# Two causal attention layers: the value products one step further behind the scores, with four buffers of probabilities

## The reference, cut to what matters

```python
# third layer: 16 heads of 8
logits = einsum('bhsd,bhtd->bhst', q, k) / sqrt(8)      # causal mask
probs = softmax(logits); out = einsum('bhst,bhtd->bhsd', probs, v) @ w_out.T
# fourth layer: 16 heads of 8, and one rotary part of 32 shared by all heads
c = x @ W_kv_down; k = c @ W_k_up; v = c @ W_v_up; q = x @ W_q
scores = (einsum('bqhd,bkhd->bhqk', q, k) + rotary(x @ W_q_rope) . rotary(c @ W_k_rope)) / sqrt(40)
attn = softmax(causal(scores)) @ v; out = attn @ W_o
```

## Time and profile before

| | us |
|---|---|
| median of 3 runs (lowest, highest) | 2511.58 (2503.85, 2516.45) |
| the profiled execution | 2516.36 |
| its span, first to last instruction | 2514.2 |
| A2: first to last subtraction of line 768 | 1201.7 to 1597.5 |
| A3: first to last subtraction of line 768 | 1853.6 to 2285.6 |
| mean granted TensorE clock, share of full speed | 0.844 |

### The profile page before, as it was taken

The page is one execution under the profiler, slowest core; times in us unless marked ns, Lnnn a source line. Parts: engine busy times, 40 slices in busy tenths (PEclk is TensorE's granted clock), DMA queues, the critical chain, the costliest instruction groups (busy, mean ns, idle before and its releaser), DMA issues.

```text
span 2514.2 us, 61783 instructions
## 1 busy us (share of the span) xinstructions
PE 1907.0 (76%) x21198; PEld 1363.1 (54%) x21199; DVE 1575.3 (63%) x3649; ACT 1221.9 (49%) x2607; POOL 1139.9 (45%) x921
## 2 busy tenths in 40 slices
PE   1553799999999788805888888683768787777998
PEld 0223466666667566604566666462535555555666
DVE  2236788787888788856444444475655555554774
ACT  0232577676777555501555555552235455554553
POOL 0003477675555233320775555342036775543551
PEclk9785799999999899955677776696777878988999
DMA  8900000011000011120111113021043333420223
GB/s 228 178 0 0 11 17 17 18 40 46 2 2 2 26 47 47 57 71 19 51 53 33 32 30 94 17 60 56 1 105 98 99 104 92 104 79 26 62 63 116
DMA packets 165195, 138.38 MB, mean 55 GB/s; under 512 B 17128, under 2 KB 151368, under 8 KB 164976
## 3 DMA queue, kind: packets, MB, share of 16 engines
q1 hardware_dynamic: 151312, 107.24, 17.2%
q0 software_dynamic: 11584, 23.91, 2.8%
q10 hardware_dynamic: 2080, 4.19, 0.5%
HBM read 57.84 MB, written 52.01 MB: 44 GB/s over the span
## 4 chain that ended last, share of the span: by engine, by line
PE 47%; DVE 20%; issue 11%; POOL 11%; ACT 8%; DMA 2%; DVEq 1%; SPq 1%; ACTq 0%; POOLq 0%
PE duo L1167 12%; PE mo L1167 9%; POOL v L768 7%; PE ob L1167 7%; PE misc L1167 7%; PE acc L1167 6%; PE pt L1167 3%; ACT v L1040 3%; DVE nmax L2288 2%; ACT v L1039 2%; DVE v L1973 2%; DVE region L2291 1%; DVE v L1965 1%; POOL rstd L736 1%; DVE stats L1795 1%
## 5 line engine op out<-in xcount | busy, mean ns | idle before, releaser
L768 POOL TENSOR_TENSOR v<-v 128x768 f16<-128x768 f32 x256 | 419.7, 1640 | 461.6 <-ACT v L1040 459.6
L763 POOL TENSOR_TENSOR v<-v 128x512 f16<-128x512 f32 x256 | 290.5, 1153 | 257.1 <-DVE region L2291 256.8
L790 POOL DMA_INDIRECT results<-probT,dest_no x202 | 217.2, 1075 | 329.8 <-ACT probT L822 289.3
L1167 PE MATMUL ob<-wm,v 128*128 128x9 f16 (+1 forms) x5856 | 257.4, 180 | 107.5 <-POOL v L768 86.3
L1167 PEld LDWEIGHTS ob<-wm,v 128*128 128x128 f16 x5856 | 215.3, 99 | 190.6 <-POOL v L768 93.7
L2180 DVE TENSOR_REDUCE nm<-duo 128x2 f16<-128x256 f32 x256 | 108.8, 425 | 294.8 <-PE duo L1167 294.7
L1039 ACT ACTIVATE v<-mo 128x384 f32<-128x384 f32 x352 | 174.3, 495 | 205.4 <-PE mo L1167 203.2
L1102 ACT ACTIVATE v<-mo 128x512 f32<-128x512 f32 x256 | 153.4, 599 | 157.7 <-PE mo L1167 157.7
L2288 DVE TENSOR_REDUCE nmax<-duo 128x2 f32<-128x512 f32 x256 | 164.9, 686 | 82.5 <-PE duo L1167 82.5
L1167 PE MATMUL duo<-kT,wm 128*128 128x256 f16 x1212 | 172.6, 279 | 56.0 <-DVE kT L1961 30.4
L1040 ACT ACTIVATE v<-mo 128x384 f16<-128x384 f32 x352 | 175.6, 499 | 0.0
(11 more groups left out here) (318 smaller groups left out, 4376.6 us busy)
## 6 DMA issues: line engine op xcount, KB each, us to landing
prob<-slot_rows SPq DMA_DIRECT2D x101, 130.0 KB, 2.2
head_rows<-v SPq DMA_DIRECT2D x96, 128.0 KB
load<-wm SPq DMA_DIRECT2D x32, 384.0 KB
qT<-results SPq DMA_DIRECT2D x40, 256.0 KB, 3.1
qT<-wm SPq DMA_DIRECT2D x16, 384.0 KB
slot_rows<-prob SPq DMA_DIRECT2D x4, 1300.0 KB, 19.4
slot_rows<-prob SPq DMA_DIRECT2D x4, 1235.0 KB, 19.7
kT<-head_rows SPq DMA_DIRECT2D x40, 96.0 KB
```

Of the source, the lines that this page charges most:

```text
L763: pool.tensor_tensor(p16[:, p % 2, h, 1, :], p32[:, h, :], p16[:, p % 2, h, 0, :], ALU.subtract)\
L768: pool.tensor_tensor(p16_2[:, p % 2, 1, :], p32_2[:, p % 2, :], p16_2[:, p % 2, 0, :], ALU.subtract)\
L790: pool.indirect_dma_start(out=results[layer], out_offset=bass.IndirectOffsetOnAxis(ap=dest_no[:, 2 * b + t:2 * b + t + 1], axis=0), in_=y_ ...
L1167: return pe.matmul(dst, lhsT, rhs, start=start, stop=stop)
```

## The change

The value products of step p are issued in step p + 2 instead of p + 1; the float16 probabilities get four buffers instead of two (the two new ones lie behind the values in the expert weights that are free in that stage); the float32 ones keep two. What depends on the value products moves one step back: `turn_o`, `out_proj`, `keep_o`, `add`, `scale_o`. So does all of `prepare`, and `put_rows` on SyncE. The steps at which SyncE reads the stacks back (`next_at`, `last_at`), the LEADs and the three score banks stay. The dispatch's sends in these two stages go out in every second step: those of A2 end with its fourth chunk, those of A3 with its last step.

```diff
+        N_P16 = 4
+                "p": [p16_2[:, b, :, :] for b in range(2)]
+                + [near[:, at:at + 4 * LINE].rearrange("p (n c) -> p n c", n=2)
+                   for at in (2 * n_v + 4 * CHUNK, 2 * n_v + 4 * CHUNK + 4 * LINE)]}
...
-                put_at = {2: {2: 0, 4: 1}, 3: {4: 0, 6: 1}}[layer]
+                put_at = {2: {3: 0, 5: 1}, 3: {5: 0, 7: 1}}[layer]
...
-                    pool.tensor_tensor(p16_2[:, p % 2, 1, :], p32_2[:, p % 2, :], p16_2[:, p % 2, 0, :], ALU.subtract)\
+                    both = kept[layer]["p"][p % N_P16]
+                    pool.tensor_tensor(both[:, 1, :], p32_2[:, p % 2, :], both[:, 0, :], ALU.subtract)\
...
                         n = i * STEPS + p
+                        if layer > 1:
+                            n = n // 2 if n % 2 else n_tiles
                         if n < n_tiles:
                             send_row_tile(layer, n // ALL, n % ALL)
...
-                    act.activation(p16_2[:, p % 2, 0, own], src, ACT.Exp).then_inc(p_high.sem, 1)
+                    act.activation(kept[layer]["p"][p % N_P16][:, 0, own], src, ACT.Exp).then_inc(p_high.sem, 1)
...
-                        if p == 1 and not (isinstance(i, int) and i == 0):
+                        if p == 2 and not (isinstance(i, int) and i == 0):
                             keep_o(i - 1)
...
-                                    ins = mm(ob[:, at:at + SLOT], p16_2[:, p % 2, pl, c:c + P],
+                                    ins = mm(ob[:, at:at + SLOT], after["p"][p % N_P16][:, pl, c:c + P],
...
-                        if p >= 1:
-                            average(i, parity, p - 1)
+                        if p >= 2:
+                            average(i, parity, p - 2)
                         elif begun:
-                            average(i - 1, 1 - parity, STEPS - 1)
+                            average(i - 1, 1 - parity, STEPS - 2 + p)
                         at = ahead(layer, p, more)
                         if at:
                             maxima(i + at[0], at[1])
-                        if begun and p == 1:
+                        if begun and p == 2:
                             turn_o(i - 1)
-                        if begun and p == (7 if layer == 2 else 2):
+                        if begun and p == (8 if layer == 2 else 3):
                             out_proj(i - 1)
                         if more:
                             prepare(i + 1, p)
                     if not more:
+                        average(i, parity, STEPS - 2)
                         average(i, parity, STEPS - 1)
...
-                        if p and p % 4 == 0:
+                        if p > 1 and p % 4 == 1:
                             scale_o(i, p // 4 - 1)
-                        elif p == 0 and begun:
+                        elif p == 1 and begun:
                             scale_o(i - 1, 3)
...
-                        if p == (8 if layer == 2 else 2) and begun:
+                        if p == (9 if layer == 2 else 3) and begun:
                             add(acc_full, x_made, i - 1, 0)
```

More of the change, by code:

```diff
@@ L302, in build_program @@
                 "q": [near[:, 2 * n_v + b * CHUNK:2 * n_v + (b + 1) * CHUNK] for b in range(2)],
-                "k": [near[:, 2 * n_v + (2 + b) * CHUNK:2 * n_v + (3 + b) * CHUNK] for b in range(2)]}
+                "k": [near[:, 2 * n_v + (2 + b) * CHUNK:2 * n_v + (3 + b) * CHUNK] for b in range(2)],
+                "p": [p16_2[:, b, :, :] for b in range(2)]
+                + [near[:, at:at + 4 * LINE].rearrange("p (n c) -> p n c", n=2)
+                   for at in (2 * n_v + 4 * CHUNK, 2 * n_v + 4 * CHUNK + 4 * LINE)]}
         def stack4(a):
@@ L1012, in prepare @@
                     if layer == 2:
-                        if p == 2:
+                        if p == 3:
                             parts_free(i, 0)
                             high(i, 0, 0, acc, SCALE2)
-                        if p == 3:
+                        if p == 4:
                             parts_free(i, 1)
                             high(i, 2, 1, acc, 1.0)
-                        if p == 5:
+                        if p == 6:
                             keep_values(i, parity, 2)
                     else:
-                        if p == 3:
+                        if p == 4:
                             proj_full.wait(act, stage, i, 0)
@@ L1026, in prepare @@
                             high(i, 0, 1, misc, SCALE3)
-                        if p == 5:
+                        if p == 6:
                             parts_free(i, 1)
                             high(i, 2, 4, acc, 1.0)
-                        if p == 8:
+                        if p == 9:
                             keep_values(i, parity, 7)
@@ L1411, in prepare @@
                             project(misc, w3q, xT)
-                        if p == 4:
+                        if p == 5:
                             proj_read_a.wait(pe, stage, i, 0)
                             rope(acc, 0, xT)
-                        if p == 5:
+                        if p == 6:
                             proj_read_v.wait(pe, stage, i, 0)
@@ L1419, in prepare @@
                             project(acc, w3k, cT3)
-                        if p == 6:
+                        if p == 7:
                             proj_read_v.wait(pe, stage, i, 2)
                             rope(misc, 2, cT3)
-                        if p == 7:
+                        if p == 8:
                             proj_read_v.wait(pe, stage, i, 6)
                             rope(acc, 3, cT3)
-                        if p == 8:
+                        if p == 9:
                             proj_read_v.wait(pe, stage, i, 7)
```

## The result

| | before | changed |
|---|---|---|
| median, us (lowest, highest; 4 runs each) | 2512.78 (2503.85, 2516.45) | 2328.97 (2316.93, 2333.41) |
| the profiled execution; its span | 2516.36; 2514.2 | 2333.41; 2331.3 |
| A2, first to last subtraction | 395.8 | 290.3 |
| A3, first to last subtraction | 432.0 | 351.0 |
| mean granted TensorE clock | 0.844 | 0.899 |

The ratio is 0.9266, 95% interval 0.9222 to 0.9309: 184 us less, where 117 were forecast. A2 gave 105 (76 forecast), A3 81 (41 forecast), and together they are the whole gain: outside them the profiled spans differ by 4 us.

What follows compares the result with a forecast made beforehand. The prediction took a loop of waits, closed by the position of `average` in TensorE's list, to bound both stages. A2 -76 and A3 -41 us sum to -117: 2516.4 becomes 2399, stated as 2400, range 2350 to 2475.

Steps and rivals of the forecast that it cites:

- limit (a): Maxima reductions, 1.80 us at full clock, hold the next `turn_maxima` or `maxima`: 4.35 us per A2 pair, 4.58 in A3.
- rival 3: TensorE at full clock nearly throughout both stages, as the clock rule has it: 44 us less, 2356 us; chance 0.09.
- a start at half clock: In A2's sum, 3 us for starting at half clock, beside 3 us for sends.
- the clock term: 30% of steps at half clock in both stages: 3.2 us per chunk in A2, 3.1 in A3.
- A3's preparing chunks: Seven A3 chunks in which steps also prepare the next chunk; forecast 50.7 us each.
- the stalls (c): A3: copy of turned maxima behind VectorE's rotary work holds `maxima`; TensorE idles 2.01 and 3.63 us; about 2 credited.
- Rival 2: VectorE's rotary work stopped more often by GpSimd, 14 uses at the worst: 27 us more, 2427 us; chance 0.14.
- Sends in every second step: Sends moved, not removed; A3's last send hidden behind the stage's remaining work, 3 us at most if not.
- Rivals 1, 4 and 5: 1: A2's clock stays low, 2428, chance 0.22; 4: wait only moves, 2516, 0.08; 5: late stack transfers, 2530, 0.05.

Runs made afterwards that it cites:

- the filler run: Kernel before, with two unused matmuls of 256 columns added in every A2 step ahead of the wait for the subtraction: ratio 0.9869, A2 356.1 us.

## Why the prediction was right, and where it was wrong

The direction and the mechanism were right and the time was not: 2400 forecast in a range from 2350 to 2475, 2329 measured. Point by point:

- **What bounded the kernel** (the place of `average`, 82.6 and 65.8 us before `ob`): right. Under 15 each was forecast, 11.0 and 10.7 came.
- **What is late next** (limit (a)): right, to 0.01 us in a plain pair of A2, 4.34 against 4.35.
- **The clock: the step that failed.** The prediction said of the stream at 4.35 per pair "I take that it mostly stays, and put a mean of 0.85 on both stages, between 0.81 and 0.90 of A3: 30% of the steps at half clock". Measured: 0.99 and 0.96. The term was 3.2 us per chunk in A2 and 3.1 in A3, 44 us in all, and nearly all of it was not there. Without it a chunk of A2 is 34.9 + 2.1 = 37.0 by the prediction's own sum; five of the first seven measured 37.1, one 36.0, the first 37.8. The mechanism of rival 3, given 0.09, was the case, though its 2356 was still 27 us too long. In the sum for A2: 7 x 3.2 = 22.4 for the clock, 6 for a start at half clock and for sends that cost nothing, 1.6 in the last chunk; 320.1 less these is 290.1 against 290.3. Over both stages 711 us were forecast and 641 measured: of the 70, the clock term is 44, A3's preparing chunks beyond it are 16 (below), and A2's start and sends with the last chunk of each stage are 10.
- **Why that step went wrong.** It took A3's mean clocks of 0.81 and 0.90 as a rate at which any such stream loses the clock. They were means over a stage in which TensorE waited before the value products of most steps (65.8 us) and stood in two stalls of 2.0 and 3.6 us per chunk, and the change took away both. The runs in A3 weigh them: 0.86 with both, 0.88 without the stalls, 0.93 without the wait before the value products, 0.96 with neither. So what the clock followed was above all the wait that the change was made to remove, and the prediction kept the clock of the loop while it removed the loop's wait. Nor was 97% busy at half clock evidence of density: at half clock the same matmuls last longer (four for `duo` 0.80 us, at the full clock 0.49).
- **The clock rule of rival 3.** A2 of the kernel before was at both levels, the lower one in the earlier trace rows and the full one in the earlier trace rows, with a mean of 0.70 and 82.6 us of idle time in 2304 weight loads; the changed kernel was at 1.00 in a stretch 88% busy, and the filler run at 1.00 in one 80% busy. The Trainium skill ("TensorE: Matmul & The Clock Gate", "Why this matters for your kernels") holds that a busy stream keeps the full clock and that long idle gaps lose it. The traces of the changed kernel and of the filler run agree; that of the kernel before doesn't, since its gaps were short. The same page of the Trainium skill ("A second HAM failure mode: psum-queue depth-cycling") tells of a kernel whose TensorE idles briefly and often between groups of matmuls and swings between both levels; A2 before looks like it. What no run here settles is why the 22.4 us of the earlier trace rows, with 0.66 us idle, stayed at the lower level.
- **A3's stalls: the second term mis-sized.** "About 2 of the stalls (c)" per chunk: measured 5.6 by itself and 7.1 behind the lag. For the order of the work 2 was about right (2.6). What was left out is that the stall of 3.63 us in the earlier trace rows held a meeting with GpSimd of 1.92 us, with 1.5 us more behind it at half clock. Seven chunks of 50.7 were forecast and took 45.3 on average: 3.1 of the 5.4 is the clock term and 2.3 is this, after some new waits (9.8 us before the weights of `pt`, 6.8 of them for a row of maxima).
- **Rival 2** (VectorE's rotary line stopped more often by GpSimd): the mechanism is real and its sign was the other way. It was not a risk of the change but a cost of the kernel before, in six chunks of seven, and the change removed it: 0.681 on average where it was 1.425. (The addition just ahead of it, line 2123, now 2131, is still stopped a little: 0.987 us on average before, 0.815 in the changed kernel, 0.693 with the preparation later alone.) The Trainium skill ("SBUF — State Buffer", SBUF: two separate sides) says that a VectorE instruction with two inputs in SBUF and a GpSimd one that reads SBUF take a shared port pair, each for its whole length, and that whichever starts first gets it. The trace agrees with the first half, and shows that starts 0.4 us apart in the profile may go either way. The prediction took the risk from GpSimd's busy share; the runs show that the step in which the line stands weighs more (six stops, then none). It is no rule of even steps either: with a send in every step the changed kernel had the line at 2.60 in three chunks (and the addition ahead of it at 1.88 to 2.42), which took 49.8 to 50.6 us where the chunk ahead of them took 48.5. How much of the 12 us that the thin sends are worth in A3 is this, the runs don't separate.
- **Sends in every second step**: hidden at the end, as forecast. That they are worth 29 us behind the lag and nothing without it was in no term.
- **Rivals 1, 4 and 5** did not happen: the clock in A2 rose, the new wait at the turn is 45.7 us where 82.6 went, and transfers cost single microseconds (6.8 and 5.9 us in A3).

Where the gain came from, by the runs in A3: 432.0, with the shift 392.9, with the lag too 363.3, with the thin sends 351.0. In A2: 395.8, the shift alone nothing (398.7), the lag on top 307.3, the thin sends 290.3; and by the filler, some 40 of the lag's 91 could be had by the clock alone.

## What to carry to other kernels

Where a stage shows a mean clock between the two levels, find the waits behind it, the short ones of the plain steps as well as the long stalls, and ask whether the change removes them: a change that takes them out takes out the clock term with them, and a mean of the old stage is then no guide. Here, in A3, the short waits weighed more (0.86 to 0.93 without them) than the stalls (0.86 to 0.88). A cheap test is filler matmuls in the stall; if the stage gets faster with more work, the clock is the price. When work is moved by one step in a loop that alternates, ask which side of its engine's urgent instruction it lands on, and which instruction of GpSimd it meets; one step was worth 39 us here, and two steps nothing. And once a wait has been moved off an instruction, put that instruction ahead of the wait that is late next.

## What was not expected of the hardware

- 51.4 us of additional matmuls made a stage 39.7 us shorter, by a granted clock of 0.96 instead of 0.70.
- A stream at the lower level can be 97% busy for 22.4 us without rising, and one at the full level 75% busy for 23.0 us, or 88% busy for 147 us in the changed kernel, without falling.
- A VectorE instruction of 0.68 us took 2.60 beside a GpSimd subtraction of 1.64, though it began 0.39 us before it; beginning 0.40 us before it, it was not held. After the 3.6 us for which TensorE then stood idle it ran at the lower level, so 1.9 us became 3.5. One and the same program had a stop of the rotary line (2.09 us) in one profile and none in another.
- Waits of at most 1.8 us in most steps held the mean clock of A3 lower (0.88 with them alone) than two stalls per chunk of up to 4.4 us did (0.93 with those alone).
